# State-space layer: two of sixteen states scanned into SBUF and multiplied by C on GpSimd, gate written in place

## What is computed

```
def step(h, inp):
    d_t, u_t, b_t, c_t = inp
    dA = jnp.exp(d_t[..., None] * A)
    h = dA * h + (d_t * u_t)[..., None] * b_t[:, None, :]
    y = jnp.einsum('ben,bn->be', h, c_t)
    return (h, y)
...
y = _selective_scan(xc, delta, A, Bm, Cm, D_param)
y = y * xr
return y @ W_out + b_out
```

## Time and profile before

| | us |
|---|---|
| median of 3 runs | 3575.87 |
| lowest, highest run | 3572.97, 3580.39 |
| the profiled execution's own time | 3569.94 |
| its span in the profile | 3568.1 |
| mean granted clock of TensorE | 0.905 of full |
| busy: VectorE, TensorE matmul, GpSimd, ScalarE | 2699.4, 2788.9, 1957.8, 1627.7 |

### The profile page before, as it was taken

How to read it: one execution, slowest core, us unless ns; L and a number is a source line. 1 busy time by engine, 2 the same in 40 slices (tenths; PEclk the granted TensorE clock), 3 DMA queues, 4 the chain that set the end, 5 groups by cost and what they waited for, 6 DMA issues and landing times. The chain is left out here.

```text
span 3568.1 us, 59422 instructions
## 1 busy us (share of the span) xinstructions
PE 2788.9 (78%) x18120; PEld 1772.7 (50%) x18120; DVE 2699.4 (76%) x4251; ACT 1627.7 (46%) x3050; POOL 1957.8 (55%) x1702
## 2 busy tenths in 40 slices
PE   4767777879899537877777778659999999998455
PEld 2434555546556312332333333238888888886222
DVE  3767888846534329999999999967888878887787
ACT  3535666634222135655655556423333333333565
POOL 1226777747656547777777777743333333333444
PEclk9987999979999869999999999999999999999555
DMA  5701000001155433334333333300000000000000
GB/s 187 330 0 22 18 17 16 13 14 43 42 151 160 123 117 133 129 119 143 130 126 135 131 131 130 130 14 3 3 3 3 3 3 3 3 3 2 9 18 21
DMA packets 136956, 248.05 MB, mean 70 GB/s; under 512 B 50017, under 2 KB 104822, under 8 KB 116226
## 3 DMA queue, kind: packets, MB, share of 16 engines
q1 hardware_dynamic: 121392, 223.49, 18.6%
q0 software_dynamic: 9088, 16.94, 1.4%
q10 hardware_dynamic: 6354, 6.27, 0.6%
HBM read 189.34 MB, written 59.13 MB: 70 GB/s over the span
## 5 line engine op out<-in xcount | busy, mean ns | idle before, releaser
L1741 POOL TENSOR_TENSOR s_drive<-s_du,s_b_sb 128x1024 f32<-128x1024 f32 x256 | 602.0, 2354 | 267.1 <-DVE s_state_ps L1967 266.8
L2080 PE MATMUL s_y_ps<-s_read,w_ident 128*128 128x512 f32 x1024 | 529.7, 648 | 201.6 <-DVE s_read L1981 200.4
L1967 DVE TENSOR_TENSOR_SCAN s_state_ps<-s_decay_ps,s_drive 128x512 f32<-128x512 f32 x512 | 600.3, 1218 | 105.0 <-ACT s_decay_ps L1874 59.6
L1874 ACT ACTIVATE s_decay_ps<-s_delta,neg_rate 128x508 f32<-128x508 f32 x512 | 348.2, 686 | 375.0 <-DVE s_state_ps L1967 374.8
L2080 PEld LDWEIGHTS s_y_ps<-s_read,w_ident 128*128 128x128 f32 x1024 | 193.9, 203 | 516.5 <-DVE s_read L1981 317.5
L2295 ACT ACTIVATE c_pT<-c_turn_ps 77x512 f32<-77x512 f32 x256 | 151.2, 592 | 483.8 <-PE c_turn_ps L2485 483.8
L2264 POOL TENSOR_TENSOR c_p<-c_p,c_norm 128x1232 f32<-128x1232 f32 x64 | 147.0, 2297 | 324.5 <-DVE c_norm L2377 324.5
L1981 DVE TENSOR_TENSOR s_read<-s_state_ps,s_c_sb 128x1024 f32<-128x1024 f32 x256 | 313.6, 1225 | 12.7 <-DVE s_state_ps L1967 1.4
L1360 POOL DMA_INDIRECT m_y_scratch<-e_y,e_index x156 | 152.5, 978 | 92.0 <-DVE e_y L1406 51.0
L685 ACT ACTIVATE b_pT<-b_turn_ps 77x512 f32<-77x512 f32 x256 | 145.4, 591 | 119.1 <-PE b_turn_ps L810 119.1
L619 POOL TENSOR_TENSOR b_p<-b_p,b_top 128x1232 f32<-128x1232 f32 x64 | 143.9, 2248 | 94.9 <-DVE b_top L742 94.9
(11 more groups left out here) (340 smaller groups left out, 6668.0 us busy)
## 6 DMA issues: line engine op xcount, KB each, us to landing
s_b_sb<-s_bc_scratch SPq DMA_DIRECT2D x64, 1024.0 KB, 4.7
s_c_sb<-s_bc_scratch SPq DMA_DIRECT2D x64, 1024.0 KB, 4.7
m_rows_scratch<-fill SPq DMA_DIRECT2D x33, 1040.0 KB, 26.5
e_w<-in_m_we_dram SPq DMA_DIRECT2D x39, 384.0 KB, 3.2
e_xg<-m_rows_scratch SPq DMA_DIRECT2D x39, 260.0 KB, 3.4
k_y<-m_y_scratch SPq DMA_DIRECT2D x32, 256.0 KB, 3.5
x<-in_x_dram SPq DMA_DIRECT2D x16, 256.0 KB, 2.9
out_dram<-q_result SPq DMA_DIRECT2D x16, 256.0 KB, 2.3
```

The costliest lines, as they stand in the source:

```text
L1741: nc.gpsimd.tensor_tensor(drive[:, n % 2, :, :], du[:, s, :, :], b_sb[:, n, :].unsqueeze(1).broadcast_to([128, halves, GT]), ALU.mult).the ...
L1874: nc.scalar.activation(decay[:, m, :, 1:], delta[:, s, m, :].rearrange("p (b t) -> p b t", t=T)[:, :, 1:], ACT.Exp, scale=core.neg_rate[:, ...
L1967: nc.vector.tensor_tensor_scan(state[:, h, :], decay[:, h, :, :].rearrange("p b t -> p (b t)"), drive[:, n % 2, h, :], 0.0, ALU.mult, ALU. ...
L2080: last = nc.tensor.matmul(y_ps[:, m, :], core.ident[:, :], read[:, n % deep, m, :], start=False, stop=(n == states - 1))
```

## The change

States 5 and 8 (`aside`) are scanned into a new SBUF tile `s_state_aside` instead of PSUM. VectorE does no `read_state` for them. GpSimd multiplies them by C in `read_beside`, which stands in its program after the drive of state n+2: after drive 7 for state 5 and after drive 10 for state 8, ahead of `make_delta` and the like. Two semaphores, `read_out` and `read_aside`, replace one. `gate_y` writes into `s_res_gate` itself, and `project_out` reads it there; so `gate_res`, which refills a slot, waits for `project_out` of the group two before it (o_ready) rather than for `gate_y`. The tile `s_y` goes. `drive_slots` is 2, as before. The orders of TensorE and ScalarE are as before.

```diff
@@ -1527,6 +1527,8 @@
     x = core.x
     halves, states, rank, taps = 2, 16, 16, 4
     deep = 4
+    drive_slots = 2
+    aside = (5, 8)
     chunks = 4
     per_chunk = states // chunks
     rows_bc, rows_dt = slice(0, 2 * states), slice(2 * states, 2 * states + rank)
@@ -1565,9 +1567,9 @@
         du = sb("s_du", [128, 2, halves, GT])
         b_sb = sb("s_b_sb", [128, states, GT])
         c_sb = sb("s_c_sb", [128, 2, per_chunk, GT])
-        drive = sb("s_drive", [128, 2, halves, GT])
+        drive = sb("s_drive", [128, drive_slots, halves, GT])
+        state_aside = sb("s_state_aside", [128, halves, GT])
         read = sb("s_read", [128, deep, halves, GT])
-        y = sb("s_y", [128, halves, GT])
         soft = conv_sig
         bc_dram = nc.dram_tensor("s_bc_scratch", [NG, 2 * states, GT], F32, kind="Internal").ap()
 
@@ -1606,12 +1608,28 @@
         decay_ready = sig("s_decay_ready", 2 * states)
         driven = sig("s_driven", states)
         scanned = sig("s_scanned", 2 * states)
-        read_out = sig("s_read_out", states)
+        read_out = sig("s_read_out", states - len(aside))
+        read_aside = sig("s_read_aside", len(aside))
         skipped = sig("s_skipped")
         summed = sig("s_summed", states)
         y_ready = sig("s_y_ready")
         o_ready = sig("s_o_ready")
         x_steps = sig("s_x_steps", 2)
+
+        def wait_read(eng, g, n):
+
+            if n in aside:
+                eng.wait_ge(read_aside.sem, read_aside.at(g, aside.index(n) + 1))
+            else:
+                before = sum(m not in aside for m in range(n + 1))
+                eng.wait_ge(read_out.sem, read_out.at(g, before))
+
+        def wait_chunk_read(eng, g, c):
+
+            own = range(per_chunk * c, per_chunk * (c + 1))
+            for group in ([n for n in own if n in aside], [n for n in own if n not in aside]):
+                if group:
+                    wait_read(eng, g, group[-1])
 
         def ahead(g, n):
 
@@ -1649,9 +1667,9 @@
             def load_c(g, c):
                 slot = c_in[c % 2]
                 if c >= 2:
-                    sp.wait_ge(read_out.sem, read_out.at(g, per_chunk * (c - 1)))
+                    wait_chunk_read(sp, g, c - 2)
                 elif behind(g, 1):
-                    sp.wait_ge(read_out.sem, read_out.at(g - 1, per_chunk * (c + 3)))
+                    wait_chunk_read(sp, g - 1, c + 2)
                 sp.wait_ge(slot.sem, slot.at(g, 16 * (c // 2)))
                 own = slice(states + per_chunk * c, states + per_chunk * (c + 1))
                 sp.dma_start(c_sb[:, c % 2, :, :].rearrange("p n t -> p (n t)"),
@@ -1711,7 +1729,7 @@
             def gate_res(g, s):
                 pool.wait_ge(res_open.sem, res_open.at(g, 1))
                 if behind(g, 2):
-                    pool.wait_ge(y_ready.sem, y_ready.at(g - 1, 0))
+                    pool.wait_ge(o_ready.sem, o_ready.at(g - 2, 1))
                 nc.gpsimd.tensor_tensor(res_gate[:, s, :, :], res_sig[:, :, :], res[:, :, :],
                                         ALU.mult).then_inc(res_ready.sem, 1)
 
@@ -1734,17 +1752,29 @@
                 if n % per_chunk == 0:
                     own = b_in[n // per_chunk]
                     pool.wait_ge(own.sem, own.at(g, 16))
-                if n >= 2:
-                    pool.wait_ge(scanned.sem, scanned.at(g, 2 * n - 2))
+                if n >= drive_slots:
+                    pool.wait_ge(scanned.sem, scanned.at(g, 2 * (n - drive_slots + 1)))
                 elif behind(g, 1):
-                    pool.wait_ge(scanned.sem, scanned.at(g - 1, 2 * (states + n) - 2))
-                nc.gpsimd.tensor_tensor(drive[:, n % 2, :, :], du[:, s, :, :],
+                    pool.wait_ge(scanned.sem, scanned.at(g - 1, 2 * (states + n - drive_slots + 1)))
+                nc.gpsimd.tensor_tensor(drive[:, n % drive_slots, :, :], du[:, s, :, :],
                                         b_sb[:, n, :].unsqueeze(1).broadcast_to([128, halves, GT]),
                                         ALU.mult).then_inc(driven.sem, 1)
+
+            def read_beside(g, n):
+                pool.wait_ge(scanned.sem, scanned.at(g, 2 * n + 2))
+                c = n // per_chunk
+                slot = c_in[c % 2]
+                pool.wait_ge(slot.sem, slot.at(g, 16 * (c // 2 + 1)))
+                pool.wait_ge(summed.sem, summed.at(g, n - deep + 1))
+                nc.gpsimd.tensor_tensor(read[:, n % deep, :, :], state_aside[:, :, :],
+                                        c_sb[:, c % 2, n % per_chunk, :].unsqueeze(1).broadcast_to(
+                                            [128, halves, GT]), ALU.mult).then_inc(read_aside.sem, 1)
 
             def body(g, s):
                 for n in range(states):
                     drive_state(g, s, n)
+                    if n - 2 in aside:
+                        read_beside(g, n - 2)
                     if n == 1 and ahead(g, 1):
                         gate_u(g + 1, 1 - s)
                     if n == 3 and ahead(g, 1):
@@ -1960,12 +1990,22 @@
 
             def scan_state(g, s, n):
                 dve.wait_ge(driven.sem, driven.at(g, n + 1))
-                if n or behind(g, 1):
-                    dve.wait_ge(read_out.sem, read_out.at(g, n))
+                if n in aside:
+                    into = state_aside
+                    if n == aside[1]:
+                        wait_read(dve, g, aside[0])
+                    elif behind(g, 1):
+                        wait_read(dve, g - 1, aside[1])
+                else:
+                    into = state
+                    if n:
+                        wait_read(dve, g, max(m for m in range(n) if m not in aside))
+                    elif behind(g, 1):
+                        wait_read(dve, g - 1, states - 1)
                 for h in range(halves):
                     dve.wait_ge(decay_ready.sem, decay_ready.at(g, 2 * n + h + 1))
-                    nc.vector.tensor_tensor_scan(state[:, h, :], decay[:, h, :, :].rearrange("p b t -> p (b t)"),
-                                                 drive[:, n % 2, h, :],
+                    nc.vector.tensor_tensor_scan(into[:, h, :], decay[:, h, :, :].rearrange("p b t -> p (b t)"),
+                                                 drive[:, n % drive_slots, h, :],
                                                  0.0, ALU.mult, ALU.add).then_inc(scanned.sem, 1)
 
             def read_state(g, s, n):
@@ -1974,7 +2014,7 @@
                     dve.wait_ge(summed.sem, summed.at(g, n - deep + 1))
                 elif behind(g, 1):
                     dve.wait_ge(summed.sem, summed.at(g - 1, states + n - deep + 1))
-                if n % per_chunk == 0:
+                if n % per_chunk == 0 or n - 1 in aside:
                     c = n // per_chunk
                     slot = c_in[c % 2]
                     dve.wait_ge(slot.sem, slot.at(g, 16 * (c // 2 + 1)))
@@ -1986,9 +2026,7 @@
             def gate_y(g, s):
                 dve.wait_ge(summed.sem, summed.at(g, states))
                 dve.wait_ge(res_ready.sem, res_ready.at(g, 1))
-                if behind(g, 1):
-                    dve.wait_ge(o_ready.sem, o_ready.at(g, 0))
-                nc.vector.tensor_tensor(y[:, :, :], y_ps[:, :, :], res_gate[:, s, :, :],
+                nc.vector.tensor_tensor(res_gate[:, s, :, :], y_ps[:, :, :], res_gate[:, s, :, :],
                                         ALU.mult).then_inc(y_ready.sem, 1)
 
             def leave_group(g, s):
@@ -2005,7 +2043,8 @@
             def body(g, s):
                 for n in range(states):
                     scan_state(g, s, n)
-                    read_state(g, s, n)
+                    if n not in aside:
+                        read_state(g, s, n)
                     if n == 0 and behind(g, 1):
                         gate_y(g - 1, 1 - s)
                     if n == 4 and behind(g, 1):
@@ -2075,7 +2114,7 @@
                 last.then_inc(skipped.sem, 1)
 
             def sum_state(g, s, n):
-                pe.wait_ge(read_out.sem, read_out.at(g, n + 1))
+                wait_read(pe, g, n)
                 for m in range(halves):
                     last = nc.tensor.matmul(y_ps[:, m, :], core.ident[:, :], read[:, n % deep, m, :],
                                             start=False, stop=(n == states - 1))
@@ -2091,7 +2130,7 @@
                     pe.wait_ge(x_steps.sem, x_steps.at(g - 1, 1))
                 for j in range(GB):
                     for m in range(halves):
-                        last = nc.tensor.matmul(f1_ps[:, j * 128:(j + 1) * 128], y[:, m, j * 128:(j + 1) * 128],
+                        last = nc.tensor.matmul(f1_ps[:, j * 128:(j + 1) * 128], res_gate[:, s, m, j * 128:(j + 1) * 128],
                                                 core.w["s_w_out"][:, m, :], start=(m == 0), stop=(m == halves - 1))
                 last.then_inc(o_ready.sem, 1)
```

## The result

The kernel after takes 3693.3 us (median of 4 runs, 3688.1 to 3705.6) against 3575.4 for the kernel before (now the median of 4): ratio 1.0333, interval 1.0305 to 1.0361. The prediction was 3690 us. The profiled execution took 3688.1 us, with a span of 3686.3, 118.2 more than before.

A forecast was written before the change was run, and what follows sets the result against it. A second chain, read 5 to scan 8, was taken to end last already, not VectorE. 52 + 29 - 3 + 24 + 15 - 3 = +114 on 3569.9, plus 5.9 for the median: 3690 us, range 3636 to 3732.

The forecast's parts named there:

- The chain: Start of scan 5 to scan 8: late sum 5 delays project_dt, take_raw and decay 8, 3.5 a body, +52 us.
- my two cases: Start of scan 5 to scan 8: 15.15 us, or 2.1 more if the low clock holds through sum 5 and project_dt.
- rival A: TensorE's low clock stays in all chains, as in body 13: 3729 us; chance 0.12.
- The conv term: Scans 12 and 13: late, slow sum 8 delays project_conv's halves and decays 12 and 13, 1.7 a body, +24 us.
- the 15: Low clock lasting longer on TensorE in a third of the bodies, for both sums: +15 us, bounds 0 and +54.
- the other end (+3): Scans 12 and 13 if sum 8 runs at TensorE's high clock: +3 us instead of +24.
- Rival B: TensorE's clock stays high: +56 us in all, 3632 us; chance 0.08.
- The gate: On GpSimd gate_res waits for project_out, drive 4 queues behind it and scan 4 slips: +29 us.
- Rival D: gate_res's wait is covered, project_out coming some 2.4 us earlier relative to drive 3: 3661 us; chance 0.07.
- State 8: Scan 8 to scan 10: decay 10 behind soft_ln lets only 0.2 of 1.54 us arrive, -3 us over 15 bodies.
- The 0.28: At the start of scan 8: no longer waiting for read 7 saves VectorE 0.28 us a body.
- +114: Sum of all terms over the kernel, in us: 52 + 29 - 3 + 24 + 15 - 3.

The follow-up runs named there:

- e4: The kernel after with project_dt moved ahead of sum 5 in TensorE's order: 3562.3 us, ratio 0.9957 to the kernel before.
- e5: The kernel after with matmuls of zeros filling TensorE's idle time ahead of sums 5 and 8: 3646.9 us, ratio 1.0194.
- e1: The kernel before with gate_y in place and gate_res waiting for project_out, no state aside: 3603.0 us, ratio 1.0056.
- e7: The kernel after with gate_res moved behind drive 4 instead of drive 3 on GpSimd: 3670.0 us, ratio 1.0260.
- e9: e8 with soft_ln moved behind decay 10 instead of decay 9 on ScalarE: ratio 0.9860 on another chip.
- e10: The kernel before with project_dt ahead of sum 5 and project_conv ahead of sum 8, no state aside: ratio 0.9960 on another chip.
- e8: The kernel after with project_dt ahead of sum 5, project_conv ahead of sum 8 and gate_res behind drive 4: 3522.0 us, ratio 0.9837.
- e3: The kernel after with state 8 alone aside: 3635.3 us, ratio 1.0146.

## Why the prediction was right

*The chain.* The decisive reading was that S8 was already ended by read 5, sum 5, `project_dt`, `take_raw` and decay 8, and not by VectorE, whose work the change takes. Measured, sum 5 came at S5+7.12 (predicted 7.1), and decay 8, which stands behind `take_raw`, ended VectorE's idle time before S8 in 15 bodies. e4 shows the cause, not only the size.

*Sizes.* S5 to S8 was 15.7 to 15.9 in six bodies and 17.3 in nine (with 15.15 and 17.3 as my two cases). The clock's share was mis-sized there: I had the long low spell (rival A) in a third of the bodies, it came in nine of fifteen. The conv term with its clock was 34.3 where 24 and part of the 15 gave about 34, but not as I had it: S10 to S13 grew by 3.0 in seven bodies, where sum 8 took 3.78 (six of them behind 6.2 us of idle TensorE), and by 1.9 in the seven in which it took 2.6 to 2.8 behind 4.1 to 4.2. And the first half of `project_conv`, which I had at the high clock (3.60), took 4.4 to 4.7 in all 14. That this makes 34 as well is in part luck. e5 prices the low clock in both stretches at 67 us, and leaves the conv term at +3.2, the other end (+3) that the prediction gave for it. Rival B, that the clock stays high, did not come: sum 5 took 3.78 in all bodies. The idle spell was 4.8 to 5.4 us before it, not 6.8, because sum 4 ran low as well (3.41 in body 11).

One reading in the prediction was wrong: not every idle spell above 3 us was followed by slow matmuls. In the kernel before, sum 5 of body 15 took 1.98 behind 3.02. The length of the spell alone does not decide: `skip` of body 12 took 3.53 behind 2.54 before and 1.98 behind 2.53 after.

*The gate.* +29 predicted, +23.8 measured. The term has two values in turn, 2.6 and 1.2, for my 2.0 and 2.4: in body 12, and so in turn, `skip` ran at the high clock (1.98 us), and `project_out` ended 8.6 behind the start of `gate_y` where it had been 10.2; in body 11 it ended 10.1 behind it, for 9.9 before. Rival D did not come; e1 and e7 show the wait from both sides.

*State 8.* -3 for S10 held (S8 to S10 is 7.46 for the predicted 7.47), and e9 shows that `soft_ln` is what held it.

*Not foreseen.* S0 to S3 and S13 to S15 became 5.6 us shorter together. Of this, 2.6 come from the looped bodies, where a state that is not aside takes 3.72 us from scan to scan instead of 3.80 at most places, and 3.0 from S14 to S15, which was 4.15 in every second looped body and is 3.72. Both appear in all kernels with a state aside and in neither e1 nor e10. The cause stays open; that it lies in how the scan's wait for the read is written or counted there would fit and was not tried. The 0.28 that S8 was to gain by not waiting for read 7 is 0.15 (S7 to S8 is 3.65 in e8, for 3.80), but S5 to S8 is 9.61 there all the same, as the prediction had it (9.6). VectorE's waits for the decay came to 217.5 us where I had some 130 and more: 107.1 at S8, 46.7 at the start of the stage, and 63.7 for the most part at S10, S12 and S13.

Errors of -5 at S4 and -6 here met +13 at the chains, so that the stage's +116.8 comes so near to +114 is in part luck.

## What to carry to other kernels

Before work is moved off the busiest engine, ask at each place whether that engine or a second chain ends last, and what is queued behind the consumer of the moved result. A result that comes 3.5 us later in an engine's strict order delays all that stands behind its consumer, wanted or not; moving those instructions ahead of it (two lines here) turned +3.3% into a gain of 0.4%, and with every engine's queue read the same way the kernel is 2.1% faster than before.

## What the runs showed of the hardware

A stall elsewhere can move TensorE's bursts to either level of its clock. In e1, with 14 late gates, sum 5 ran at the high level in bodies 1 to 14 and sums 4 and 8 at the low one; in e3 the bodies 4 to 12 took in turn 10.97 and 13.81 us from S5 to S8. Work of zeros worth 6 us kept the granted clock at 1.00 in the 3.7 us behind it. The scan's price hardly depends on where it writes: 1209 ns into SBUF, 1216 into PSUM. With two multiplies more on GpSimd, neither it nor VectorE slowed down (2355 and 2352 ns for a drive, 1225 and 1224 for a read).
